# Three linked edits in a four-layer graph network kernel: layer 3's matrix, minus mean over deviation, and the order of work

## The chip, the cores and the metric

The kernel runs on one core of a Trainium2 chip. The metric is the device time of one execution in microseconds (us). Three executions of the kernel before gave 1169.11, 1172.59 and 1173.3 us, so the median is 1172.59 us.

## What is computed

There are 128 graphs of 128 nodes with 128 features. Four layers follow each other, each ending in a residual and a layer norm:

```python
x = _layernorm(x + _L0(x, adj, ...))   # adj @ x + eps0*x, W1 (128x512), rms norm, silu, W2
x = _layernorm(x + _L1(x, ...))        # conv1 (1 tap), conv2 (17 taps), exp(-distance) @ relu(msg), GRU gates
x = _layernorm(x + _L2(x, adj, ...))   # h = x @ W', then 3 hops: adj/row_sum @ ., leaky relu

def _L3_gnn_ref(x, adj, eps, W1, b1, W2, b2):
    aggregated = jnp.einsum('bnm,bmd->bnd', adj, x)
    h = (1.0 + eps) * x + aggregated
    h = jax.nn.relu(h @ W1 + b1)
    return h @ W2 + b2
x = _layernorm(x + _L3(x, adj, ...))
```

`(1+eps)*x + adj @ x` is computed as one product with the matrix `adj + (1+eps)*I`, which is what this document calls layer 3's matrix. A layer norm is applied by ScalarE as `y*rstd + nm`, where `nm` is minus the mean times `rstd`, that is, minus the mean over the deviation.

## The kernel before, in words

Four graphs make a group, and there are 32 groups, numbered k. A tile holds one group: 128 partitions x 512 columns of f32. The program has three phases. Each phase is written as a loop over turns t, and in turn t every engine runs a hand-ordered list of stages, each on its own group: `stage(name, t - d)` works on group t - d if there is such a group. The order of the stages in each engine's list is the order in which that engine executes, and semaphores (`until`, `free`, `landed`) join the lists. So a stage that has to wait holds up everything behind it on its engine. A larger d is a deeper software pipeline: the first turns then have less work and the last ones more.

- **Phase one** (TensorE's loop in lines 534 to 550, 43 turns): layer 0 and the first convolution. `neighbours` (line 417) multiplies with the adjacency matrix to which GpSimd's `add_eps` (1278) has added eps0 times the identity. ScalarE and VectorE split the result into a high and a low part (`high`, `low`) for products of three matmuls (`split_product`, 149). `gram`, `product`, `square_sums`, `mean_square`, `rms`, `spread_rms` make the rms norm, `hidden` and `down` the two weight products, `x1_t`, `conv1` and `transform` what phase two needs. `row_sums` (1041) sums the rows of the adjacency matrix, which is loaded once more as `ad`.
- **Phase two** (568 to 573, 34 pairs of slots): the 17-tap convolution as products in the Fourier domain.
- **Phase three** (733 to 757, 41 turns): layers 1 to 3. `codes`, `distances`, `messages`, `gather` are layer 1's attention-like part, `inverse` returns from the Fourier domain, `hidden_n`, `gate_x`, `gate_nmp`, `gate_conv` make the gates, `y1_t` and `prop_in` start layer 2, `hop1` to `hop3` are its three hops, and `gather3`, `hidden3`, `down3` are layer 3. GpSimd's `add_eps3` (1362) makes layer 3's matrix `at3` from the adjacency matrix `atc` in every turn. VectorE's `moments` and GpSimd's `norm` (1293) give `rstd`, VectorE's `minus_mean` (1223) gives `nm`, and ScalarE's `apply2` (917) and `apply3` (926) apply the norms of layers 2 and 3.

The eight banks of PSUM hold one group's product each and are shared by several stages in turn; the `free(...)` calls say whose reader must be done first. `distances` (591) writes into banks 0 to 3 at once. In the kernel before it waits, through bank 2, for VectorE's `agg3` (1229, tile `agg_lo`, line 1232) of group k - 7:

```python
free(pe, ("agg3_hi agg3_lo", k - 7), ("msg", k), ("z1", k - 8), ("edge", k - 1))
```

VectorE's list in phase three has before that `agg3`, in the same turn: `hop(t-5, 3)`, `points(t, 1)`, `minus_mean(t-6, 0)` and `stats3(t-8)`. All DMAs are issued by SyncE, in one list per phase.

Of the kernel before, what the change touches and what calls it, by code (L numbers as in the profile page):

```python
# [45 lines left out]
ae nb agg agg_hi agg_lo gram prod sums ms r_rms spread rv hid0 hid1 hid2 hid3 hn0 hn1 hn2 hn3  # L46
# [12 lines left out]
y2 moments2 r2 nm2 x3_rows x3b at3 agg3_ps agg3_hi agg3_lo z_ps0 z_ps1 z0 z1 y3_ps y3  # L59
moments3 r3 nm3 out_rows  # L60
# [4 lines left out]
def graph_layers(nc, w, out):  # L65
    with ExitStack() as ctx:
# [6 lines left out]
        X_RING, AT_RING, AD_RING, X1_RING = 4, 2, 2, 2  # L73
# [10 lines left out]
        X1C_RING, ATC_RING, YH_RING, OUT_RING = 4, 8, 2, 2  # L84
# [5 lines left out]
        x1_dram = nc.dram_tensor("x1_scratch", [GROUPS, P, G, P], F32, kind="Internal").ap()  # L90
        yh_dram = nc.dram_tensor("yh_scratch", [SLOTS, B, 2 * P], F32, kind="Internal").ap()
# [89 lines left out]
        eps0_ident = sb("eps0_ident", [P, P])  # L181
# [46 lines left out]
        eps3_ident = sb("eps3_ident", [P, P])  # L228
        one_eps3 = sb("one_eps3", [P, 1])
# [16 lines left out]
        y2, x3_rows, x3b, at3 = rows("y2"), rows("x3_rows"), rows("x3b"), rows("at3")  # L246
# [4 lines left out]
        nm = [sb(f"nm{i}", [P, G]) for i in range(2)]  # L251
# [3 lines left out]
        TURNS1 = GROUPS + 11  # L255
# [7 lines left out]
        DVE_B1_SQ, DVE_BN_VE, DVE_CONV1, DVE_EPS0, DVE_READY = 1, 2, 6, 7, 15  # L263
# [3 lines left out]
        ACT_LATE, DVE_PROP, DVE_LATE = ACT_READY + 4, DVE_TAPS + 10, DVE_TAPS + 14  # L267
# [12 lines left out]
        def everything_first(engine):  # L280
# [23 lines left out]
        def _(sp):  # L304
# [35 lines left out]
            for t in range(TURNS1):  # L340
# [3 lines left out]
                stage(store_x1, t - 6)  # L344
                stage(load_ad, t + 2 - 11)
# [70 lines left out]
        def _(pe):  # L416
            def neighbours(k):
                until(pe, "ae", k)
                landed(pe, x_in, k)
# [1061 lines left out]
```

## Time and profile before

| | |
|---|---|
| median of three executions | 1172.59 us |
| the profiled execution | 1173.6 us |
| its span, first to last instruction | 1171.8 us |
| mean granted TensorE clock | 0.985 |
| busy: TensorE matmul, weight load | 94%, 84% of the span |
| busy: VectorE, ScalarE, GpSimd | 71%, 59%, 48% |
| chain that ended last | TensorE 81%, VectorE 9%, issue 6% |
| read and written in HBM | 55.31 MB, 25.69 MB |

The profiled execution is 1.8 us longer than its span, and 1.0 us over the median. A matmul's duration in the trace includes the pipeline, so matmuls overlap and a TensorE that is shown 100% busy may still have small gaps; distances from start to start tell more. In a timeline row the columns are start, duration (both us), engine, line, operation, tiles and shapes, count, and in square brackets the idle time before it with what ended it.

### The profile page before, as it was taken

Reading aid. Unit: us, or ns where it says so; the run is one execution under the profiler, and the core shown is the slowest. Engines: PE = TensorE matmul, PEld = TensorE weight load, DVE = VectorE, ACT = ScalarE, POOL = GpSimd, SP = SyncE. Lnnn points to the kernel's source line nnn. Section 1 sums busy time; section 2 is a strip of 40 time slices with the busy share of each in tenths; the row PEclk is TensorE's granted clock in tenths of the full one; section 3 lists DMA queues with packets and bytes.
Section 4 is the critical chain, followed back from the end, with each engine's and each line's share of the span. In section 5 each row is a group of like instructions: output and inputs, shape, how many; then the busy total and the mean of one; then the engine's idle time right before and its main releaser. Section 6 shows DMA issues by size and latency. Waiting matters only on the chain.

```text
span 1171.8 us, 25210 instructions
## 1 busy us (share of the span) xinstructions
PE 1102.7 (94%) x8267; PEld 990.0 (84%) x8267; DVE 833.5 (71%) x2596; ACT 694.8 (59%) x1296; POOL 563.0 (48%) x524
## 2 busy tenths in 40 slices
PE   7899999999999789899999999999999999999874
PEld 6799999999999679788888888888888888888774
DVE  4477778787777533146887778877787878877974
ACT  4444555555555332256677777767776776767665
POOL 1244433434342235335555555656555565656654
PEclk9999999999999899899999999999999999999998
DMA  4122332223232255411111121211212121220000
GB/s 156 55 64 75 99 91 91 91 91 91 91 91 64 73 168 180 155 50 58 34 40 54 47 65 47 65 38 47 65 47 65 47 65 40 64 65 10 20 28 36
DMA packets 47110, 82.62 MB, mean 71 GB/s; under 512 B 5316, under 2 KB 15368, under 8 KB 46728
## 3 DMA queue, kind: packets, MB, share of 16 engines
q1 hardware_dynamic: 46984, 81.02, 22.5%
q8 instruction: 69, 1.13, 0.4%
q14 instruction: 57, 0.47, 0.1%
HBM read 55.31 MB, written 25.69 MB: 69 GB/s over the span
## 4 chain that ended last, share of the span: by engine, by line
PE 81%; DVE 9%; issue 6%; ACT 2%; DMA 1%; SPq 0%; POOL 0%; DVEq 0%; POOLq 0%; ACTq 0%
PE banks L156 16%; PE banks L465 9%; PE banks L150 9%; PE banks L151 8%; PE banks L152 8%; PE banks L722 4%; PE banks L631 3%; PE banks L632 3%; PE banks L493 3%; PE banks L558 2%; PE banks L609 2%; PE banks L435 2%; DVE stats L1019 2%; DVE prop L1214 2%; PE banks L587 2%
## 5 line engine op out<-in xcount | busy, mean ns | idle before, releaser
L163 POOL TENSOR_TENSOR rstd<-ve,minus_half 128x4 f32<-128x4 f32 x128 | 130.5, 1020 | 101.9 <-DVE ve L1029 98.8
L163 POOL TENSOR_TENSOR r_rms<-ms,minus_half 128x4 f32<-128x4 f32 x32 | 32.3, 1008 | 224.2 <-DVE ms L993 224.2
L465 PE MATMUL banks<-w,s 128*128 128x128 f32 x768 | 101.2, 275 | 0.4 <-DVE y L1007 0.4
L465 PEld LDWEIGHTS banks<-w,s 128*128 128x128 f32 x768 | 95.6, 192 | 3.4 <-issue 0.5
L150 PE MATMUL banks<-agg_hi,w_hi 128*128 128x512 f32 x192 | 82.4, 429 | 10.1 <-issue 8.6
L1373 POOL TENSOR_TENSOR y<-leaky,x_rows 128x512 f32<-128x512 f32 x32 | 42.6, 1331 | 97.3 <-ACT x_rows L922 96.8
L1019 DVE BATCH_NORM_STATS2 stats<-y 128x6 f32<-128x128 f32 x384 | 82.9, 278 | 1.7 <-POOL y L1373 1.6
L1359 POOL TENSOR_TENSOR x3b<-x_rows,late_rows 128x512 f32<-128x512 f32 x32 | 40.9, 1278 | 82.5 <-DVE y L1239 82.5
L160 ACT ACTIVATE agg_hi<-banks 128x512 fp32r<-128x512 f32 x64 | 38.2, 597 | 64.7 <-PE banks L156 36.1
L151 PE MATMUL banks<-agg_lo,w_hi 128*128 128x512 f32 x192 | 76.4, 398 | 0.0
L152 PE MATMUL banks<-agg_hi,w_lo 128*128 128x512 f32 x192 | 76.3, 398 | 0.0
L156 PE MATMUL banks<-at,x_rows 128*128 128x128 f32 x512 | 69.8, 281 | 4.4 <-DVE agg_lo L981 3.0
L156 PE MATMUL banks<-t,atc 128*128 128x128 f32 x512 | 68.8, 278 | 1.3 <-DVE t L1214 1.3
L722 PE MATMUL banks<-w,z 128*128 128x128 f32 x512 | 69.5, 282 | 0.2
L781 ACT ACTIVATE s<-hn,cols 128x512 f32<-128x512 f32 x96 | 65.0, 712 | 7.7 <-DVE hn L1000 7.7
L1000 DVE SCALAR_TENSOR_TENSOR hn<-banks,cols,rv 128x512 f32<-128x512 f32 x96 | 68.2, 736 | 1.0 <-ACT rv L160 0.6
L156 PEld LDWEIGHTS banks<-at,x_rows 128*128 128x128 f32 x512 | 63.9, 196 | 5.3 <-issue 2.9
L722 PEld LDWEIGHTS banks<-w,z 128*128 128x128 f32 x512 | 64.4, 198 | 1.3 <-ACT z L943 1.3
L156 PEld LDWEIGHTS banks<-t,atc 128*128 128x128 f32 x512 | 63.0, 194 | 1.9 <-DVE t L1214 1.9
L1159 DVE SCALAR_TENSOR_TENSOR c_res<-banks,bn_scale,x1c 128x512 f32<-128x512 f32 x32 | 24.0, 751 | 52.0 <-PE banks L632 52.0
L930 ACT ACTIVATE out_rows<-y,nm,rstd 128x128 f32<-128x128 f32 x128 | 52.5, 483 | 11.8 <-DVE nm L1226 11.7
L1315 POOL TENSOR_SCALAR y<-wh 128x128 f32<-128x128 f32 x67 | 34.3, 530 | 47.8 <-ACT xh L160 25.7
(192 smaller groups left out, 3401.1 us busy)
## 6 DMA issues: line engine op xcount, KB each, us to landing
at<-in_at SPq DMA_DIRECT2D x32, 256.0 KB, 2.9
x_rows<-in_x SPq DMA_DIRECT2D x32, 256.0 KB, 2.9
x_scratch<-x SPq DMA_DIRECT2D x32, 256.0 KB, 3.2
ad<-in_ad SPq DMA_DIRECT2D x32, 256.0 KB, 2.7
x1c<-x_scratch SPq DMA_DIRECT2D x32, 256.0 KB, 2.7
atc<-in_at SPq DMA_DIRECT2D x32, 256.0 KB, 2.9
yh<-yh_scratch SPq DMA_DIRECT2D x32, 256.0 KB
out<-out_rows SPq DMA_DIRECT2D x32, 256.0 KB, 3.1
```

The lines of the kernel that those rows point to most:

```text
L150: pe.matmul(psum, hi, moving_hi, start=start, stop=False)
L151: pe.matmul(psum, hi, moving_lo, start=False, stop=False)
L152: return pe.matmul(psum, lo, moving_hi, start=False, stop=stop)
L156: last = pe.matmul(psum[:, g, :], lhs(g), rhs(g), start=True, stop=True)
L163: return nc.gpsimd.tensor_tensor(to[:], base[:], minus_half[:], ALU.pow)
L465: last = pe.matmul(bank[7][:, g, :], s[c][:, g, :], w2[:, c, :], start=(c == 0 and g == 0), stop=(c == H0 - 1), skip_group_check=True)
L722: last = pe.matmul(bank[6][:, g, :], z3[c][:, g, :], w32[:, c, :], start=(c == 0 and g == 0), stop=(c == H3 - 1), skip_group_check=True)
L781: nc.scalar.activation(s[c][:], hn[c][:], ACT.Silu, scale=column("rms", c)).then_inc(sem[("s0", "s1", "s2", "s3")[c]], 1)
L930: last = nc.scalar.activation(out_rows[k % OUT_RING][:, g, :], y3[:, g, :], ACT.Identity, bias=nm[1][:, g:g + 1], scale=rstd[3][:, g:g + 1])
L1000: V.scalar_tensor_tensor(out=hn[c][:], in0=bank[(5, 0, 1, 3)[c]][:], scalar=column("b1", c), in1=rv[:], op0=ALU.add, op1=ALU.mult).then_in ...
L1019: last = V.bn_stats(stats[n][:, g, :], y[:, g, :])
L1373: Q.tensor_tensor(y2[:], leaky[:], x2_rows[:], ALU.add).then_inc(sem["y2"], 1)
```

## The change

1. Layer 3's matrix. `add_eps3` moves to GpSimd's list of phase one, ahead of `add_eps`, and writes one tile `at3_made`. SyncE stores it to a scratch tensor in HBM (`store_at3`) and loads it back in phase three (`load_at3`) into a ring of two.
2. `minus_mean` moves from VectorE to GpSimd, as two instructions (times -1, then times the mean), each followed by a semaphore.
3. The lists of all engines in phases one and three have another order, with other distances d and another assignment of PSUM banks. Phase one has 42 turns where it had 43. In phase three the gates' products with the neighbours and the convolution go from t - 1 to t - 2, the three hops and layer 3's `hidden3` one turn later too; the number of turns stays 41. Rings: `x1c` 4 to 6, `atc` 8 to 11, `ad` 2 to 1.

The diff, cut to its core (the two small setup instructions for the matrix move with it, and the bank numbers change everywhere):

```diff
-        X_RING, AT_RING, AD_RING, X1_RING = 4, 2, 2, 2
+        X_RING, AT_RING, AD_RING, X1_RING = 4, 2, 1, 2
-        X1C_RING, ATC_RING, YH_RING, OUT_RING = 4, 8, 2, 2
+        X1C_RING, ATC_RING, YH_RING, OUT_RING = 6, 11, 2, 2
-        TURNS1 = GROUPS + 11
+        TURNS1 = GROUPS + 10
...
+            def store_at3(k):
+                until(sp, "at3", k)
+                sp.dma_start(at3_dram[k], at3_made[:]).then_inc(at3_stored, 16)
...
                 stage(load_at, t + 2)
                 if t >= 2:
                     stage(load_x, t + 1)
-                stage(store_x1, t - 6)
-                stage(load_ad, t + 2 - 11)
+                stage(store_at3, t - 0)
+                stage(store_x1, t - 5)
+                stage(load_ad, t + 1 - 9)
...
+            def load_at3(k):
+                until(sp, "agg3_ps", k - 2)
+                landed(sp, at3_in, k - 2)
+                sp.dma_start(at3[k % 2][:], at3_dram[k]).then_inc(at3_in[k % 2], 16)
...
             def distances(k):
                 until(pe, "pts_l", k)
                 until(pe, "pts_r", k)
-                free(pe, ("prop", k - 5), ("v", k - 2), ("edge", k - 1))
-                free(pe, ("factor_r pts_r", k), ("t2", k - 5), ("edge", k - 1))
-                free(pe, ("agg3_hi agg3_lo", k - 7), ("msg", k), ("z1", k - 8), ("edge", k - 1))
-                free(pe, ("xn_hi xn_lo", k - 1), ("z0", k - 8), ("edge", k - 1))
+                free(pe, ("factor_r pts_r", k), ("y3", k - 9), ("edge", k - 1))
+                free(pe, ("tz", k - 2), ("edge", k - 1))
+                free(pe, ("t2", k - 5), ("ht", k - 5), ("edge", k - 1))
+                free(pe, ("ghn", k - 1), ("prop", k - 6), ("t1", k - 6), ("edge", k - 1))
...
             def y1_t(k):
-                free(pe, ("x2_rows", k - 1))
+                free(pe, ("msg", k + 4), ("x2_rows", k - 1))
```

TensorE's new lists, in full:

```python
# phase one
hidden(t-1, 0)  neighbours(t)  square_sums(t-1)  hidden(t-1, 2)  hidden(t-1, 3)  down(t-2, 0)
spread_rms(t-1)  down(t-2, 1)  gram(t)  conv1(t-7)  down(t-2, 2)  transform(t-9, 1)
x1_t(t-4)  hidden(t, 1)  down(t-2, 3)  transform(t-9, 0)
# phase three
codes(t)  hop3(t-6)  gate_nmp(t-2, R)  gate_nmp(t-2, N)  gate_conv(t-2, R)  gate_nmp(t-2, Z)
gate_conv(t-2, N)  hop1(t-5)  hidden_n(t-1)  gate_conv(t-2, Z)  inverse(t)  distances(t)
hidden3(t-8, 0)  gather(t-1)  messages(t)  prop_in(t-4)  y1_t(t-4)  hidden3(t-8, 1)
down3(t-8, 0)  hop2(t-5)  down3(t-8, 1)  gate_x(t-1, Z)  gather3(t-7)  gate_x(t-1, R)
```

VectorE's, ScalarE's and GpSimd's new lists of phase three, and GpSimd's of phase one:

```python
# VectorE
hop(t-6, 3)  agg3(t-8)  points(t, 0)  twice_x(t-3)  moments(t-9, 3)  gate_u(t-2)  points(t, 1)
gate_v(t-2)  hop(t-5, 1)  stats2(t-6)  apply1(t-5)  conv_residual(t)  moments(t-6, 2)
nmp_low(t-1)  stats1(t-4)  moments(t-4, 1)  hop(t-5, 2)  residual3(t-8)  scaled_h(t-4)
twice_n(t-2)  stats3(t-8)
# ScalarE
factors(t, 0)  factors(t, 1)  multiple(t-5, 3)  apply2(t-7)  gate_r(t-2)  leaky_relu(t-6)
multiple(t-5, 2)  hidden_n(t-1)  conv_high(t-1)  gate_z(t-2)  x1_high(t)  multiple(t-5, 0)
edges(t)  nmp_high(t-1)  message(t)  hidden3(t-8, 0)  multiple(t-5, 1)  conv_full(t)
hidden3(t-8, 1)  apply3(t-9)  gate_n(t-2)  agg3(t-7)
# GpSimd
edge_weights(t-1)  residual2(t-6)  x1_low(t)  conv_low(t-1)  norm(t-9, 3)  minus_mean(t-9, 1)
twice_y1(t-3)  norm(t-6, 2)  norm(t-4, 1)  minus_mean(t-6, 0)  x3_bias(t-7)
# GpSimd, phase one
add_eps3(t)  add_eps(t)  rms(t-1)  norm(t-3, 0)  x_bias(t-2)
```

```diff
+            def add_eps3(k):
+                landed(pool, at_in, k)
+                if k >= 1:
+                    pool.wait_ge(at3_stored, 16 * k)
+                Q.tensor_tensor(at3_made[:], at[k % AT_RING][:], over_graphs(eps3_ident), ALU.add
+                                ).then_inc(sem["at3"], 1)
...
+            def minus_mean(k, n):
+                until(pool, ("r2", "r3")[n], k)
+                Q.tensor_scalar(minus_rstd[n][:], rstd[2 + n][:], -1.0, None, ALU.mult
+                                ).then_inc(sem[("minus_r2", "minus_r3")[n]], 1)
+                until(pool, ("minus_r2", "minus_r3")[n], k)
+                Q.tensor_tensor(nm[n][:], minus_rstd[n][:], mv[2 + n][:, :, 0], ALU.mult
+                                ).then_inc(sem[("nm2", "nm3")[n]], 1)
```

VectorE's new list of phase one is `stats0(t-3)`, `mean_square(t-1)`, `moments(t-3, 0)`, `conv1_bias(t-8)`, `low(t)`, `row_sums(t-9)`, `normalise(t-1, 1)`, `normalise(t-1, 0)`, `product(t)`, `normalise(t-1, 3)`, `apply0(t-3)`, `residual0(t-2)`, `normalise(t-1, 2)`.

## Rows read from the trace of the kernel before

**Rows 1.** The page: its span, and busy us (share) and count per engine.
```profile
span 1171.8 us, 25210 instructions
PE 1102.7 (94%) x8267; PEld 990.0 (84%) x8267; DVE 833.5 (71%) x2596; ACT 694.8 (59%) x1296; POOL 563.0 (48%) x524
```

**Rows 2.** Windows: stretch, length, busy PE, PEld, DVE, ACT, POOL, granted clock, DMA share, GB/s.
```profile
29.50:119.10 89.60, 86.55 (x600) 79.08 (x601) 59.92 (x156) 42.62 (x67) 36.02 (x32) 1.00 0.24 68
119.10:373.60 254.50, 254.50 (x1916) 236.52 (x1915) 193.52 (x506) 135.63 (x242) 98.11 (x89) 1.00 0.29 88
373.60:424.30 50.70, 38.02 (x273) 34.77 (x272) 28.02 (x74) 21.71 (x44) 7.44 (x7) 0.93 0.25 81
...
485.10:594.20 109.10, 105.95 (x791) 90.23 (x791) 66.20 (x182) 67.86 (x121) 50.39 (x40) 0.97 0.20 60
594.20:1083.80 489.60, 475.10 (x3602) 418.67 (x3602) 387.72 (x1344) 348.06 (x669) 285.31 (x240) 0.99 0.18 52
1083.80:1171.80 88.00, 62.10 (x411) 55.40 (x409) 65.56 (x268) 53.77 (x109) 47.13 (x40) 0.91 0.08 28
```

**Rows 3.** Timeline of TensorE, phase one: `neighbours` of two turns that follow each other.
```profile
176.92 1.06 PE L156 MATMUL banks<-at,x_rows 128*128 128x128 f32 x8
...
188.49 1.06 PE L156 MATMUL banks<-at,x_rows 128*128 128x128 f32 x8
```

**Rows 4.** Timeline of TensorE, a turn of phase three, from `codes` to `codes`.
```profile
820.43 0.65 PE L587 MATMUL banks<-x1c,code_w 128*32 128x128 f32 x16
...
825.80 1.06 PE L156 MATMUL banks<-t,atc 128*128 128x128 f32 x8
826.70 1.06 PE L156 MATMUL banks<-at,x_rows 128*128 128x128 f32 x8
827.51 0.48 PE L150 MATMUL banks<-x_hi,wt_hi 128*128 128x512 f32 x1
...
828.29 0.40 PE L150 MATMUL banks<-x_hi,wt_hi 128*128 128x512 f32 x1
...
830.15 0.40 PE L152 MATMUL banks<-xn_hi,wt_lo 128*128 128x512 f32 x1
831.13 0.50 PE L600 MATMUL banks<-points_lr 9*128 9x128 f32 x8 [0.57 <-DVE agg_lo L1232]
...
840.67 0.53 PE L587 MATMUL banks<-x1c,code_w 128*32 128x128 f32 x12
```

**Rows 5.** Line 600 (`distances`): what ended its waits, us and times.
```profile
  DVE agg_lo L1232: 14.5, 24
```

**Rows 6.** Timeline of VectorE ahead of that wait.
```profile
828.20 1.20 DVE L1226 SCALAR_TENSOR_TENSOR nm<-mv,rstd 128x4 f32<-128x4 f32 x1
```

**Rows 7.** Timeline of TensorE: a stretch at the lower clock in phase three.
```profile
647.88 1.91 PE L156 MATMUL banks<-w3h,atc 128*128 128x128 f32 x8
```

**Rows 8.** Tile `nm`: VectorE's `minus_mean`, ns min/median/max, first and last start.
```profile
L1226 DVE SCALAR_TENSOR_TENSOR nm<-mv,rstd x64: 143/191/1235, 566.9 to 1167.5; 128x4 f32<-128x4 f32 x64
```

**Rows 9.** The page, costliest groups: GpSimd's power on 128x4, and its one-input 128x128.
```profile
L163 POOL TENSOR_TENSOR rstd<-ve,minus_half 128x4 f32<-128x4 f32 x128 | 130.5, 1020 | 101.9 <-DVE ve L1029 98.8
...
L1315 POOL TENSOR_SCALAR y<-wh 128x128 f32<-128x128 f32 x67 | 34.3, 530 | 47.8 <-ACT xh L160 25.7
```

**Rows 10.** Groups by line, GpSimd, 800 to 1000 us: `add_eps3`.
```profile
L1365 POOL TENSOR_TENSOR at<-atc,eps_ident 128x512 f32<-128x512 f32 x9 | 11.6, 1288 | 0.0
```

**Rows 11.** DMA issues: count, KB each, median us from issue to landing.
```profile
x_scratch<-x SPq DMA_DIRECT2D x32, 256.0 KB, 3.2
ad<-in_ad SPq DMA_DIRECT2D x32, 256.0 KB, 2.7
```

**Rows 12.** Timeline of TensorE, last turns of phase one.
```profile
410.29 1.13 PE L156 MATMUL banks<-conv_w,x 128*128 128x128 f32 x8 [1.67 <-DVE hcp L1039]
...
414.02 1.13 PE L156 MATMUL banks<-conv_w,x 128*128 128x128 f32 x8 [1.67 <-DVE hcp L1039]
```

**Rows 13.** Timeline of TensorE, first turn of phase three: `inverse`.
```profile
490.71 0.69 PE L631 MATMUL banks<-idft,yh 68*128 68x128 f32 x2 [1.41 <-DMA yh<-yh_scratch]
```

More of the change, by code:

```diff
@@ L245, in graph_layers @@
         t2, t1, prop, leaky = rows("t2"), rows("t1"), rows("prop"), rows("leaky")
-        y2, x3_rows, x3b, at3 = rows("y2"), rows("x3_rows"), rows("x3b"), rows("at3")
+        y2, x3_rows, x3b = rows("y2"), rows("x3_rows"), rows("x3b")
+        at3 = [rows(f"at3_{i}") for i in range(2)]
         agg3_hi, agg3_lo = rows("agg3_hi", F32R), rows("agg3_lo", F32R)
@@ L432, in square_sums @@
                 until(pe, "prod", k)
-                free(pe, ("xh1", k - 9), ("hn2", k - 1), ("ms", k - 1))
+                free(pe, ("y0", k - 2), ("ms", k - 1))
                 for g in range(G):
-                    last = pe.matmul(bank[1][:, 0, g:g + 1], agg[:, g, :], ones[:, 0:1], start=True, stop=True)
+                    last = pe.matmul(bank[0][:, 0, g:g + 1], agg[:, g, :], ones[:, 0:1], start=True, stop=True)
                 last.then_inc(sem["sums"], 1)
@@ L462, in down @@
                 if c == 0:
-                    free(pe, ("y0", k - 1))
+                    free(pe, ("ms", k + 1), ("y0", k - 1))
                 for g in range(G):
-                    last = pe.matmul(bank[7][:, g, :], s[c][:, g, :], w2[:, c, :], start=(c == 0 and g == 0),
+                    last = pe.matmul(bank[0][:, g, :], s[c][:, g, :], w2[:, c, :], start=(c == 0 and g == 0),
                                      stop=(c == H0 - 1), skip_group_check=True)
@@ L550, in _ @@
                 stage(down, t - 2, 1)
+                stage(gram, t)
+                stage(conv1, t - 7)
+                stage(down, t - 2, 2)
+                stage(transform, t - 9, 1)
+                stage(x1_t, t - 4)
+                stage(hidden, t, 1)
+                stage(down, t - 2, 3)
+                stage(transform, t - 9, 0)
             def slot_product(psum, slot):
@@ L719, in down3 @@
                 if c == 0:
-                    free(pe, ("c2_res", k + 7), ("ghn", k + 6), ("y3", k - 1))
+                    free(pe, ("edge", k + 8), ("factor_r pts_r", k + 8), ("y3", k - 1))
                 for g in range(G):
-                    last = pe.matmul(bank[6][:, g, :], z3[c][:, g, :], w32[:, c, :], start=(c == 0 and g == 0),
+                    last = pe.matmul(bank[0][:, g, :], z3[c][:, g, :], w32[:, c, :], start=(c == 0 and g == 0),
                                      stop=(c == H3 - 1), skip_group_check=True)
@@ L1038, in conv1_bias @@
                 until(dve, "hc", k - 1)
-                V.tensor_tensor(hcp[:], bank[4][:], over_graphs(conv1_b), ALU.add).then_inc(sem["hcp"], 1)
+                V.tensor_tensor(hcp[:], bank[6][:], over_graphs(conv1_b), ALU.add).then_inc(sem["hcp"], 1)
             def row_sums(k):
```

360 lines of the change are left out of this document (173 added, 187 removed).

## The prediction

> **What bounds the kernel now.** I read the page first: TensorE is busy for 94% of the span, VectorE for 71%, ScalarE for 59%, GpSimd for 48% [rows 1]. So time can come only from TensorE's work, from its gaps, or from the ends of the phases. The windows by stretch split the span into phase one's first ten turns (89.60 us), its full turns (254.50) and its last turns (50.70), then, after phase two (from 424.30 to 485.10), phase three's first eight turns (109.10), its 24 full turns (489.60) and its end (88.00) [rows 2]. 29.5 us of set-up come before them. In phase one's full turns TensorE is busy all the time, 254.50 of 254.50 [rows 2], and two starts of `neighbours` are 188.49 - 176.92 = 11.57 us apart [rows 3]. Reading one such turn from start to start I found no gap: 11.57 us is TensorE's own work, and no order makes it shorter.
>
> In phase three a turn takes 840.67 - 820.43 = 20.24 us [rows 4], and there is a gap. The last matmul before `distances` starts at 830.15 and `distances` at 831.13 [rows 4], 0.98 us, where neighbours of that kind follow in 0.23 (828.29 is three matmuls after 827.51, at 0.32 + 0.23 + 0.23). So 0.74 us are lost in each of the 24 full turns. What ended them is VectorE's `agg_lo`, 24 times, 14.5 us as the profile counts idle time [rows 5]. Ahead of `agg_lo` VectorE ran `minus_mean`, a 128x4 instruction that took 1.20 us [rows 6]; the same instruction takes 0.143 at best and 1.235 at worst [rows 8]. I looked at all 64: in every full turn the one for layer 2 takes 1.18 to 1.20, the one for layer 3 0.15. The long one of [rows 6] runs until a GpSimd instruction of 1.3 us, which had started 0.12 before it, ends. That is 1.05 us in VectorE's queue right ahead of what TensorE waits for, more than the 0.74 lost.
>
> **The change part by part.**
>
> *Phase three, full turns.* In the new lists `distances` no longer waits for layer 3's `agg_lo`; bank 6 holds that. I laid the new TensorE list out against the clock with the old steps: a fp32 product of eight matmuls 0.90 (825.80 to 826.70), 0.81 before a split product, a split product 0.78 after fp32 and 0.70 after another [rows 4]. The change of kind costs nothing on balance (0.08 more on one side, 0.09 less on the other), although there are seven such changes in the new list where there were three. The sum of one turn is 20.24 - 0.74 = 19.5 us, as before without the gap. Then I laid the other engines beside it, offsets from `codes`. ScalarE: `factors` to 1.5, `multiple` 2.1, `apply2` 3.7, `gate_r` 4.5 when its product ends, `leaky` 5.0, `hidden_n` 7.5, `conv_high` 8.1, `gate_z` 8.7. `distances` is due at 9.2 and needs `tz`: 0.4 us to spare. VectorE: `hop3` to 2.8, `agg3` 3.3, `points` done by 5.7 (3.5 to spare), `apply1` 9.4 where `messages` at 11.3 needs it, `hop2` 17.6, last `stats3` 20.2, that is 0.7 into the next turn, where `hop3` is not ready before 1.7. GpSimd is idle for some 4 us. The tightest joint is bank 7: `y1_t` is due at 13.4 and `message`, which must have emptied the bank, ends at 13.3. I take 0.05 for it. So 24 turns x 19.55 = 469.2 in place of 489.60, and of this stretch's two spells at the lower clock (one starts at 647.88, where eight matmuls take 1.91 instead of 1.06 [rows 7]; granted clock 0.99 [rows 2]; 1.75 us each in the length of their turns) I keep one: 471, **-18.6 us**, from 0 (another gap of the same size) to -21 (no gap, no such spell).
>
> *minus_mean on GpSimd.* VectorE loses 0.15 + 1.20 a turn. GpSimd gains four small instructions. The trace has no such one: the nearest are the power on 128x4, 1.02, and a one-input 128x128, 0.53 [rows 9]. I take 0.5 each, 2.0 a turn; at 1.02 it is 4.1. Against it stands `add_eps3`, 1.29, which leaves phase three [rows 10]. With 1.02 each, `nm` for `apply2` is ready 0.7 into the turn and wanted at 2.1, so at either price it is covered in a full turn. Not in the last turn of the program, where `moments`, `norm`, `nm`, `apply3`, store follow each other: there it costs 0.9 to 1.9 us. The second of them waits for the first on the same engine, a semaphore's time, inside these prices.
>
> The Trainium skill (SBUF - State Buffer, section on who interferes with whom) says that GpSimd and a VectorE instruction with two inputs in SBUF lock each other out of a shared port for the whole instruction. The trace agrees: `minus_mean` is such an instruction, and lasts 1.20 or 0.15 as GpSimd is busy or not. By that rule VectorE's `gate_u`, `twice_x` and `twice_n` can be held up too; that is priced below as a rival.
>
> *Layer 3's matrix in phase one.* GpSimd gets 1.29 us a turn more [rows 10], on 98.11 us busy of 254.50 [rows 2], and it writes before `neighbours(t)` can start. The loop is: `neighbours(t)` ends, SyncE issues `load_at`, `load_x` and `store_at3` (0.4 to 0.5 each), the store lands 3.2 after its issue (the like store of x1, [rows 11]), `add_eps3(t+1)` 1.29, `add_eps(t+1)` 1.3. That is 0.2 + 1.0 + 3.2 + 2.6 + 0.9 for `neighbours` itself, 7.9 us, under 11.57: nothing in full turns, with `x_bias`, `norm` and `rms` done before. In turns 1 and 2, which are shorter than that, it costs some 2 us. The store and the reload add 8.4 MB each; DMA engines are busy for 29% of phase one and 18% of phase three [rows 2], and SyncE's list waits for nothing new that TensorE needs within a turn. Nothing.
>
> *Phase one's order.* The pipeline is one turn shallower, so early turns hold more work. With the same unit steps the new turns 0 to 9 are 6.4, 7.1, 9.5, 9.4, 9.9, 9.9, 9.9, 10.8, 10.8 and 11.6 = 95.3, and 2 for the store loop, 97.5 against 89.60: **+8**. Full turns: the same work; `square_sums` loses a start that a split product before it gave (0.08 a turn at most): 22 turns, 0 to +1.8, I take **+1**. End: before, 50.70 us with TensorE at clock 0.93 [rows 2]; its late turns are a loop of 3.72 us (410.29 to 414.02) in which `conv1` waits 1.67 for VectorE's `hcp` [rows 12]. New: two turns of 9.3 and 7.2 with layer 0's rest, one of 4.9, then turns of 4.2. These last are now set by `ad`, whose ring of one makes load (2.7, [rows 11]), issue and row sum (0.68) a loop of 4.2 and stands ahead of `hcp` in VectorE's list. 9.3 + 7.2 + 4.9 + 4 x 4.2 + 4.5 = 42.7: **-8**, from -12 to 0. Phase two: same work, **0**.
>
> *Phase three's ends.* Start: the first turn gets worse, since `inverse` waits for its data until 490.71 [rows 13] and `distances` and `messages`, which were done in that wait, now stand behind it: 11 us for 9.2. The turns after hold less (gates one turn later): 7.2, 11.7, 11.7, 13.0, 14.8, 15.7, 16.6. Sum 101.7 against 109.10: **-7.4**, from -10 to -3. End: the 8.9 us of work that the start lost come here, 63 us of TensorE work where there were 54. I went through the nine turns: 15.4, 12.5, 12.8, 11.6, 8.8, 7.2, 5.8, and 13.4 for the last group to its store, 87.5 us, against 88.00. The old turns waited for VectorE, which waited for GpSimd's `norm` before `minus_mean`; the new ones are full with work. A clock of 0.91 [rows 2] and joints that I drew without slack make it worse: I take **+1.5**, from -3 to +8.
>
> **Sum.** +8 + 1 - 8 + 0 - 7.4 - 18.6 + 1.5 = -23.5 us. The profiled execution took 1173.6 (span 1171.8 and 1.8 around it), which is 1.0 above the median of 1172.6. So 1149 us.
>
> **The rivals.**
> - *The gap only moves* (12%). In place of `agg_lo`, `distances` waits for `tz`, or `y1_t` for `message`, for 0.7 us in each full turn. For it: 0.4 and 0.1 us to spare in a plan by hand, six more semaphore joints on TensorE. Against: ScalarE has 14 us of work in 19.5. Then the 18.6 shrink to 2, and the time is 1173 - 7 = 1166.
> - *Ports* (8%, inside the forecast's range). GpSimd holds up `twice_x` and `gate_u` by 1.2 us each. `apply1` then ends at 11.8, and `messages`, due at 11.3, waits 0.5: 24 x 0.5 = 12 us, 1161. Against: GpSimd waits for `leaky` in just that stretch. By the skill's rule above this is where it would bite.
> - *Slower than before* (7%): ScalarE's queue before `gate_z`. `apply2` waits for `nm` from GpSimd, and behind it stand `gate_r`, `leaky`, `hidden_n`, `conv_high`, `gate_z`, and for `tz` the whole of TensorE. If `nm` comes 1.4 + 0.4 + x us later than I have it, each full turn loses x. To eat the 23.5 us, x must be 1.0 us over 24 turns; at x = 1.4 the time is 1173 - 23.5 + 34 = 1183. That needs 3 us more on GpSimd than at the highest price of the trace.
> - *The ends give more* (8%): no lower clock in the late turns, `ad` hidden, shorter joints: -12 more, 1137.
> - *The change does not do what it says*: the gap's cause stays because another stage waits for `agg3`. In the new lists `hidden3` does, 6 us later. I give it nothing of its own.
>
> **How the numbers follow.** Forecast as summed: 65%, about 1149, by itself 1141 to 1158. The range reaches to the gap that only moves and to most of the better ends: 1137 to 1166. A measurement of this kernel tells about 0.5% from no change, 5.9 us. Under 1166.7 lie the forecast, the ports, the better ends and half of the moved gap, 0.86; within 5.9 of the old time the rest of the moved gap and a little of the bad tail, 0.08; slower 0.06.
>
> **What would show it.** Right: TensorE's starts of `codes` 19.5 to 19.6 us apart in turns 8 to 31 and no idle time ahead of `distances`; `minus_mean` short on GpSimd, 0.5 or less each; phase two's first matmul near 425 us; the last `codes` about 26 us earlier. Wrong: turns above 20, a wait of TensorE for ScalarE's `tz` or `message`, an end of phase one over 48 us, or an end of phase three over 95.

## The result, and the profile after

The changed kernel takes 1163.78 us (median of 20 executions, 1162.28 to 1169.23), the kernel before beside it 1172.94 (20 executions). The ratio is 0.9935, 95% interval 0.9922 to 0.9949: 9.2 us less. The forecast was 23.5 us less. The sign and the range held; the size did not. Three of the runs below had one execution each that took far longer (1599, 3141 and 2213 us), which their medians and ratios leave out.

The page of the changed kernel ([rows 1] has that of the kernel before):

```profile
span 1162.0 us, 25279 instructions
PE 1102.8 (95%) x8267; PEld 993.2 (85%) x8267; DVE 805.2 (69%) x2532; ACT 701.2 (60%) x1296; POOL 604.2 (52%) x652
```

TensorE's busy time is what it was. VectorE has 28 us less. GpSimd has 41 us more: 27.7 are the 128 small instructions of part 2 (by the groups of GpSimd, 64 of 0.233 and 64 of 0.201 us), 15.3 are two old instructions that take longer in the new order, `edge_weights` (1.63 us for 1.29) and `residual2` (1.47 for 1.33); others are a little shorter.

The same stretches as [rows 2], in the windows view of the changed kernel (stretch, length, busy PE, PEld, DVE, ACT, POOL, granted clock, DMA share, GB/s). Phase two is here too:

```profile
29.60:127.10 97.50, 93.86 (x644) 85.22 (x645) 63.21 (x167) 45.30 (x73) 51.67 (x44) 1.00 0.29 95
127.10:381.60 254.50, 254.50 (x1915) 239.40 (x1915) 187.91 (x507) 135.48 (x243) 124.90 (x108) 1.00 0.34 112
381.60:425.80 44.20, 30.70 (x228) 28.20 (x228) 22.44 (x63) 18.56 (x39) 6.65 (x7) 0.96 0.24 78
425.80:486.40 60.60, 59.50 (x407) 55.82 (x407) 17.07 (x30) 12.10 (x21) 34.98 (x69) 1.00 0.53 182
486.40:589.90 103.50, 98.33 (x740) 83.79 (x741) 53.98 (x154) 61.98 (x107) 42.95 (x37) 0.95 0.26 79
589.90:1062.90 473.00, 472.71 (x3602) 418.08 (x3602) 375.28 (x1289) 353.49 (x670) 289.54 (x313) 1.00 0.20 64
1062.90:1162.00 99.10, 72.37 (x462) 63.30 (x460) 70.18 (x286) 61.21 (x122) 49.83 (x68) 0.91 0.12 41
```

Set against [rows 2] and against the terms of the sum:

| stretch | before | after | difference | forecast |
|---|---|---|---|---|
| phase one, first ten turns | 89.60 | 97.50 | +7.9 | +8 |
| phase one, full turns | 254.50 | 254.50 | 0 | +1 |
| phase one, end | 50.70 | 44.20 | -6.5 | -8 |
| phase two | 60.80 | 60.60 | -0.2 | 0 |
| phase three, start | 109.10 | 103.50 | -5.6 | -7.4 |
| phase three, 24 full turns | 489.60 | 473.00 | -16.6 | -18.6 |
| phase three, end | 88.00 | 99.10 | **+11.1** | **+1.5** |

Six of the seven terms are within 2 us of what was summed. The last is off by 9.6 us, two thirds of the miss of 14.3 (23.5 less 9.2). Most of the rest lies in the end of phase one and in phase three's start and full turns, 1.5 to 2.0 us too little gain in each. The signs that the prediction had named point the same way: right were no wait ahead of `distances` and phase two from 425.8 us; short were turns of 19.69 us for 19.5 to 19.6 and the last `codes` 20.4 us earlier for 26; and an end of phase three over 95 us had been named as a sign of being wrong.

The gap is gone. TensorE's timeline of a full turn, from `codes` (line 601) over the last of `inverse` and `distances` (line 614) to the next `codes`, answers to [rows 4]:

```profile
806.61 0.65 PE L601 MATMUL banks<-x1c,code_w 128*32 128x128 f32 x16
...
815.55 0.39 PE L646 MATMUL banks<-idft,yh 68*128 68x128 f32 x2
815.90 0.50 PE L614 MATMUL banks<-points_lr 9*128 9x128 f32 x8
816.33 0.50 PE L152 MATMUL banks<-agg_hi,w_hi 128*128 128x512 f32 x1
...
826.30 0.64 PE L601 MATMUL banks<-x1c,code_w 128*32 128x128 f32 x16
```

`distances` starts 0.35 us after the last pair of `inverse`, with no wait shown, where it had been 0.98. The turn is 826.30 - 806.61 = 19.69 us. The two small instructions of `minus_mean` on GpSimd (tile view, ns min/median/max; [rows 8] has the one of before):

```profile
L1315 POOL TENSOR_SCALAR minus_rstd<-rstd x64: 228/230/245, 574.3 to 1157.4; 128x4 f32<-128x4 f32 x64
L1318 POOL TENSOR_TENSOR nm<-minus_rstd,mv x64: 199/200/204, 574.6 to 1157.7; 128x4 f32<-128x4 f32 x64
```

### The profile page after: what moved, and what is told of

Same layout as the page of the kernel before. It is cut to its first block, busy times and chain, and to the rows that moved or that the text cites. A ratio compares the mean times of both kernels' runs of the same rounds, so it can differ in the third digit from the quotient of the medians.

```text
span 1162.0 us, 25279 instructions
## 1 busy us (share of the span) xinstructions
PE 1102.8 (95%) x8267; PEld 993.2 (85%) x8267; DVE 805.2 (69%) x2532; ACT 701.2 (60%) x1296; POOL 604.2 (52%) x652
## 4 chain that ended last, share of the span: by engine, by line
PE 89%; DVE 3%; POOL 2%; issue 2%; ACT 2%; DMA 2%; SPq 0%; ACTq 0%; POOLq 0%; DVEq 0%
PE banks L158 19%; PE banks L152 11%; PE banks L153 10%; PE banks L154 10%; PE banks L479 10%; PE banks L736 4%; PE banks L645 3%; PE banks L646 3%; PE banks L623 3%; PE banks L572 3%; PE banks L507 2%; PE banks L449 2%; PE banks L601 2%; PE banks L686 1%; PE banks L539 1%
## 5 line engine op out<-in xcount | busy, mean ns | idle before, releaser
L1357 POOL TENSOR_TENSOR x_lo<-x1c,x_hi 128x512 fp32r<-128x512 f32 x32 | 41.1, 1284 | 114.6 <-ACT x_hi L162 114.6
L1390 POOL TENSOR_TENSOR y<-leaky,x_rows 128x512 f32<-128x512 f32 x32 | 46.9, 1466 | 102.2 <-ACT leaky L929 102.2
L152 PE MATMUL banks<-agg_hi,w_hi 128*128 128x512 f32 x192 | 90.0, 469 | 9.8 <-issue 8.3
L158 PEld LDWEIGHTS banks<-at,x_rows 128*128 128x128 f32 x512 | 67.7, 195 | 7.7 <-POOL at L1295 1.7
L795 ACT ACTIVATE s<-hn,cols 128x512 f32<-128x512 f32 x96 | 67.7, 713 | 7.6 <-DVE hn L1014 7.6
L1289 POOL TENSOR_TENSOR at_made<-at,eps_ident 128x512 f32<-128x512 f32 x32 | 41.1, 1285 | 37.0 <-DMA at_scratch<-at_made 26.4
L1027 DVE TENSOR_SCALAR x_rows<-y,mv,rstd 128x128 f32<-128x128 f32 x128 | 36.1, 345 | 29.8 <-PE banks L490 29.8
```

The source lines that it names most:

```text
L152: pe.matmul(psum, hi, moving_hi, start=start, stop=False)
L158: last = pe.matmul(psum[:, g, :], lhs(g), rhs(g), start=True, stop=True)
L795: nc.scalar.activation(s[c][:], hn[c][:], ACT.Silu, scale=column("rms", c)).then_inc(sem[("s0", "s1", "s2", "s3")[c]], 1)
L1289: Q.tensor_tensor(at3_made[:], at[k % AT_RING][:], over_graphs(eps3_ident), ALU.add).then_inc(sem["at3"], 1)
L1390: Q.tensor_tensor(y2[:], leaky[:], x2_rows[:], ALU.add).then_inc(sem["y2"], 1)
```

## The experiments

Two questions: which part of the change closes the gap, and what makes the end of phase three 11 us longer. Each run is compared with the kernel before on the same chip, so between groups of runs that were made at different times it is the ratios that compare.

### The gap: one stage moved

```diff
-                stage(minus_mean, t - 6, 0)
                 stage(stats3, t - 8)
                 stage(agg3, t - 7)
+                stage(minus_mean, t - 6, 0)
```

> The kernel before with one stage moved: in VectorE's list of phase three `minus_mean(t-6, 0)` stands behind `stats3(t-8)` and `agg3(t-7)` instead of ahead of them. Nothing else changes. If the 0.74 us gap ahead of `distances` is the 1.20 us that the long `minus_mean` takes in VectorE's queue [rows 5, 6], the gap closes in all 24 full turns: turns of 19.5 to 19.7 us in place of 20.24, 13 to 18 us in all, about 1156. If the gap was set by something else in the order of the work (the banks, ScalarE's `agg3_hi`), another wait takes its place: turns above 20.0, 1168 to 1174.

Measured: 1158.19 us, ratio 0.9861 (0.9838 to 0.9884). Full turns of 19.59 us, TensorE busy for all of them (windows view), while the long `minus_mean` is still there (VectorE's timeline), now behind `agg_lo`; TensorE's timeline shows `distances` 0.32 us after the matmul before it:

```profile
595.50:1065.60 470.10, 470.10 (x3602) 414.99 (x3602) 383.08 (x1344) 347.49 (x670) 284.31 (x240) 1.00 0.18 54
...
819.49 0.68 DVE L1232 TENSOR_TENSOR agg_lo<-banks,agg_hi 128x512 fp32r<-128x512 f32 x1
820.08 1.08 DVE L1226 SCALAR_TENSOR_TENSOR nm<-mv,rstd 128x4 f32<-128x4 f32 x1
...
820.68 0.39 PE L152 MATMUL banks<-xn_hi,wt_lo 128*128 128x512 f32 x1
821.00 0.50 PE L600 MATMUL banks<-points_lr 9*128 9x128 f32 x8
```

So a long `minus_mean`, here 1.08 us in a full turn, costs nothing once it stands behind `agg_lo`. It was its place in VectorE's queue that made the gap. That one moved line gives more than the whole change.

### The gap: part 2 alone

`minus_mean` leaves VectorE's list, and in GpSimd's list of the kernel before stand:

```diff
                 stage(norm, t - 6, 2)
+                stage(minus_mean, t - 6, 0)
...
                 stage(norm, t - 8, 3)
+                stage(minus_mean, t - 8, 1)
```

> The kernel before with part 2 alone: `minus_mean` on GpSimd, each right behind its `norm`. Theory 1 (the long `minus_mean` in VectorE's queue makes the gap): turns of 19.5 to 19.7 us, 1154 to 1159, within 3 us of the run with `minus_mean` moved later; the end of phase three within 1 us of the 88.0 us of before, since two GpSimd instructions of 0.23 and 0.20 us in place of one of 0.15 on VectorE cost 0.3 us in the last turn. Theory 2 (the new order of all lists removes the gap): no change, 1170 to 1174. Theory 3 (work taken to GpSimd delays GpSimd's other stages): slower than 1174.

Measured: 1152.86 us, ratio 0.9814 (0.9789 to 0.9838), 1 us under the first theory's range. Theories 2 and 3 are out. The stretches of its phase three, start, full turns and end:

```profile
486.80:596.20 109.40, 105.91 (x791) 90.17 (x791) 66.17 (x180) 67.80 (x121) 51.23 (x44) 0.97 0.20 60
596.20:1066.40 470.20, 470.20 (x3602) 415.06 (x3602) 369.38 (x1297) 347.55 (x670) 304.84 (x336) 1.00 0.18 54
1066.40:1152.40 86.00, 60.70 (x410) 54.01 (x408) 59.86 (x253) 53.29 (x109) 52.47 (x69) 0.94 0.08 28
```

470.20 against 489.60 [rows 2], the start as before, the end 2.0 us shorter. The small instructions on GpSimd cost nothing that shows. The time is 5.3 us under that of the line moved later, where 3 at most were expected. Nearly all of it is the end of phase three, 86.0 us here and 90.8 there, with granted clocks of 0.94 and 0.90; why that end is longer no run looks into. Phase three is 665.6 us here and 675.6 in the changed kernel: the new order is 10 us longer than the old one once the gap is closed by part 2, namely 13.1 us in the end and 2.8 in the full turns, less 5.9 gained at the start.

### The gap: part 2 undone in the changed kernel

`minus_mean` is back on VectorE. In the first try layer 3's stood behind `gate_v`:

```diff
                 stage(gate_v, t - 2)
+                stage(minus_mean, t - 9, 1)
...
                 stage(hop, t - 5, 2)
+                stage(minus_mean, t - 6, 0)
```

> The changed kernel with part 2 undone: `minus_mean` back on VectorE as one instruction, in the changed order (layer 2's behind `hop(t-5, 2)`, layer 3's behind `gate_v(t-2)`). Theory A (in the changed order the gap ahead of `distances` is gone whatever `minus_mean` does, since bank 6 holds layer 3's product): turns stay at 19.7 us and the time within 3 us of the changed kernel's 1163.8. Theory B (the lock on the long `minus_mean` comes back somewhere in VectorE's queue and is seen by TensorE): up to 1.0 us a turn, up to 1180.

Measured: 1352.17 us, ratio 1.1534 (1.1506 to 1.1563). Neither theory had this. VectorE's and TensorE's timelines of one turn:

```profile
900.35 0.16 DVE L1241 SCALAR_TENSOR_TENSOR nm<-mv,rstd 128x4 f32<-128x4 f32 x1 [6.67 <-POOL rstd L165]
...
901.84 0.81 PE L614 MATMUL banks<-points_lr 9*128 9x128 f32 x8 [5.18 <-DVE t L1229]
```

GpSimd's `norm(t-9, 3)` stands behind `residual2`, `x1_low` and `conv_low` in its list, late in the turn. VectorE waited for it for 6.67 us, and `distances` for `t2` behind it for 5.18; turns were 27.3 us. So an instruction of 0.16 us holds its queue for forty times as long as it runs, because of where another engine's list puts its operand. The second try moves that stage behind `moments(t-4, 1)`:

> The changed kernel with part 2 undone as in after_nm_vector, but `minus_mean(t-9, 1)` behind `moments(t-4, 1)` in VectorE's list instead of behind `gate_v(t-2)`, where it waited 6.67 us in each turn for GpSimd's `rstd` and made turns of 27.3 us. Theory A (the changed order removes the gap by itself): turns of 19.7 us and 1162 to 1166. Theory B (the long `minus_mean` is seen again in some place): 19.8 to 20.7, 1167 to 1188. If A holds, parts 2 and 3 each remove the gap and are worth it only once.

Measured: 1165.16 us, ratio 0.9948 (0.9924 to 0.9972), which overlaps the changed kernel's. Theory A holds. Windows and tile:

```profile
595.20:1068.20 473.00, 472.72 (x3603) 418.11 (x3602) 379.40 (x1336) 356.11 (x670) 267.88 (x217) 1.00 0.20 64
...
L1241 DVE SCALAR_TENSOR_TENSOR nm<-mv,rstd x64: 149/160/220, 579.1 to 1162.9; 128x4 f32<-128x4 f32 x64
```

The full turns are 473.00 us, equal to the changed kernel's. Here `minus_mean` never meets a long GpSimd instruction (0.22 us at most), so this run doesn't say what a held one would cost in the new order. But parts 2 and 3 each close the gap without the other, and what it cost (489.60 less 473.00, or less 470.20 in the old order) comes only once.

### Part 1 alone

`add_eps3`, its store and its reload are added to the kernel before as in the diff above, ahead of `add_eps` in GpSimd's list and behind `load_x` in SyncE's, with the order of before; `add_eps3` leaves phase three, and `ad` has a ring of one and is loaded a turn later.

> The kernel before with part 1 alone: layer 3's matrix made by GpSimd in phase one, stored, and loaded back in phase three into a ring of two; the order of the stages is that of before (`ad` has a ring of one and is loaded one turn later, for the memory). It takes 1.29 us a turn from GpSimd in phase three, and GpSimd's instruction is what holds `minus_mean`. Theory 1 (the lock on `minus_mean` is `twice_y1`, which stays): the gap stays, phase three is unchanged, phase one's first two turns 1 to 2 us longer: 1172 to 1176. Rival (with `add_eps3` gone GpSimd runs `twice_y1` earlier, and it no longer meets `minus_mean`): turns of 19.5 us and 1156.

Measured: 1224.35 us, ratio 1.0424 (1.0400 to 1.0448), 50 us slower, which neither theory had. In phase three the first one held: turns of 20.24 us, 24 waits of `distances` for `agg_lo` (13.8 us), and a `minus_mean` of 1.19 us beside `twice_y1`; the rival is out. The loss is in phase one, half of it in its first ten turns (115.4 us for 89.6) and half in its full turns, which are 12.7 us instead of 11.57. SyncE's, GpSimd's and TensorE's timelines of one such turn:

```profile
246.49 0.33 SPq L317 DMA_DIRECT2D at<-in_at  x1
251.61 0.33 SPq L313 DMA_DIRECT2D x_rows<-in_x  x1
251.98 0.44 SPq L325 DMA_DIRECT2D at_scratch<-at_made  x1
...
255.39 1.27 POOL L1297 TENSOR_TENSOR at_made<-at,eps_ident 128x512 f32<-128x512 f32 x1 [0.65 <-DMA at_scratch<-at_made]
256.74 1.26 POOL L1303 TENSOR_TENSOR at<-at,eps_ident 128x512 f32<-128x512 f32 x1
...
258.06 1.16 PE L158 MATMUL banks<-at,x_rows 128*128 128x128 f32 x8 [0.94 <-POOL at L1303]
```

`load_x` waits for `y0` (as it does in the kernel before, where only the store of x1 stands behind it and nothing is late), and the store of the matrix stands behind it: issued at 251.98, 5.5 us after `load_at`, it lands 3.3 us later, and then GpSimd needs 2.6 us until `neighbours` can start. The load of `ad` is not in this loop: it was issued at 257.42, and `load_at` behind it only at 259.25, when `neighbours` had ended. In the changed kernel `load_x` is issued right behind `load_at`; there `residual0`, which makes `y0`, comes a turn earlier (SyncE again):

```profile
243.91 0.33 SPq L317 DMA_DIRECT2D at<-in_at  x1
244.35 0.37 SPq L313 DMA_DIRECT2D x_rows<-in_x  x1
244.76 0.43 SPq L325 DMA_DIRECT2D at_scratch<-at_made  x1
```

So part 1 needs phase one's new order, and the prediction's loop of 7.9 us can hold only for that order.

### Part 1 undone in the changed kernel

The matrix is made in phase three again, and phase one has its new order without the store:

```diff
                 stage(edge_weights, t - 1)
+                stage(add_eps3, t - 7)
                 stage(residual2, t - 6)
...
```

> The changed kernel with part 1 undone: GpSimd makes layer 3's matrix in phase three, between `edge_weights(t-1)` and `residual2(t-6)`, where it is idle for some 3 us in a full turn. If part 1 is worth nothing in either phase: 1160 to 1165, phase one some 1 us shorter in its first turns (97.5 to 96). If GpSimd's 1.29 us a turn back in phase three delays `residual2` or `twice_y1` so that TensorE sees it: turns above 19.8 us, 1166 to 1180.

Measured: 1165.47 us, ratio 0.9932 (0.9905 to 0.9959), no difference from the changed kernel's 0.9935. Its full turns are 19.70 us. Its first ten turns of phase one took 95.4 us, and 97.50 with the matrix. The next run, also without the matrix, took 96.4 for them, so the store loop costs 1 to 2 us, about what the prediction gave it. The matrix on GpSimd had been covered in phase three, so that moving it gains nothing.

### Phase one's order alone

The kernel before with the lists, banks and distances of phase one from the diff, without the matrix.

> The kernel before with phase one's order, banks and number of turns from the changed kernel, without the matrix in phase one. Phase one there took 97.50 + 254.50 + 44.20 us against 89.60 + 254.50 + 50.70. If the order does it and the store loop of the matrix costs nothing: +1.4 us, 1174 to 1175. If the store loop costs the 2 us that the prediction gave it in turns 1 and 2: -0.6 us, 1172 to 1173. Phase three is as before, with its gap.

Measured: 1172.41 us, ratio 0.9988 (0.9969 to 1.0007): no difference that can be told, so executions don't decide between the two sums that were expected. It agrees with the table, where phase one's +7.9 and -6.5 nearly cancel.

### The end: other banks in the late turns

```diff
+        LATE = 30
...
+        def y1_bank(k):
+            return 4 if k == LATE else 7
...
+        def in_bank(k):
+            return 1 if k >= LATE else 2
...
             def y1_t(k):
                 until(pe, "y1", k)
-                free(pe, ("msg", k + 4), ("x2_rows", k - 1))
+                if k == LATE:
+                    free(pe, ("v", GROUPS - 1))
+                else:
+                    free(pe, ("msg", k + 4), ("x2_rows", k - 2 if k > LATE else k - 1))
...
             def prop_in(k):
                 until(pe, "y1", k)
-                free(pe, ("edge", k + 4), ("t2", k - 1), ("ht", k - 1))
...
+                if k >= LATE:
+                    free(pe, ("tz", GROUPS - 1))
+                    free(pe, ("ht", k - 1))
+                else:
+                    free(pe, ("edge", k + 4), ("t2", k - 1), ("ht", k - 1))
...
```

> The changed kernel with other banks in its late turns alone: `prop_in` of groups 30 and 31 goes to bank 1 and `y1_t` of group 30 to bank 4, both free once the gates have ended; so `prop_in` no longer waits for `t2` of the group before (1.89 and 1.64 us), nor `y1_t` for `x2_rows` in that turn. Theory Tb (shared banks make the end long): the turns of `gather3` that took 15.55 and 15.43 us become 12 to 14, the end of phase three 93 to 96 in place of 99.1, time 1158 to 1161. Theory Td (VectorE's chain of the late turns, `hop2` after `t2`, sets them, whatever bank): the waits move from `prop_in` to `hop2`, time 1162 to 1165.

Measured: 1157.73 us, ratio 0.9880 (0.9854 to 0.9906), below the changed kernel's interval. What it cures, in TensorE's timeline of the changed kernel (turns 34 and 35):

```profile
1093.36 1.13 PE L158 MATMUL banks<-w3h,atc 128*128 128x128 f32 x8 [0.54 <-issue]
1096.38 0.47 PE L152 MATMUL banks<-agg_hi,w_hi 128*128 128x512 f32 x1 [1.88 <-issue]
...
1099.21 2.05 PE L158 MATMUL banks<-prop_w,y 128*128 128x128 f32 x8 [1.89 <-DVE t L1229]
...
1113.14 1.13 PE L158 MATMUL banks<-prop_w,y 128*128 128x128 f32 x8 [1.64 <-DVE t L1229]
1115.19 1.09 PE L686 MATMUL banks<-ident,y 128*128 128x128 f32 x4 [0.92 <-DVE x_rows L1212]
...
1117.36 1.91 PE L736 MATMUL banks<-w,z 128*128 128x128 f32 x8
1119.06 1.92 PE L158 MATMUL banks<-t,atc 128*128 128x128 f32 x8
```

`prop_in` (1099.21, 1113.14) waits for VectorE's `t2` of the group before, because `hop1` (1093.36), whose product `t2` is made from, and `prop_in` both use bank 2. In a full turn 6.6 us of other products lie between `hop1` and `prop_in`; when the gates have ended, only the three matmuls of `hidden3` do (1096.38). Behind `prop_in` stand `y1_t`, `hidden3`, `down3` and `hop2`, and VectorE waits for the last of these. With the other banks neither `prop_in` waits; the first still runs at the lower clock (1.83 us for 1.05), behind the wait of 1.88 that stays:

```profile
1097.82 1.83 PE L158 MATMUL banks<-prop_w,y 128*128 128x128 f32 x8
...
1109.22 1.05 PE L158 MATMUL banks<-prop_w,y 128*128 128x128 f32 x8
```

From `gather3` to `gather3` turns 34 to 36 took 15.55, 15.43 and 9.32 us, and now take 12.59, 9.80 and 10.97. The end of phase three as in the table:

```profile
1063.60:1155.80 92.20, 69.69 (x462) 61.50 (x460) 69.83 (x286) 61.23 (x122) 49.89 (x68) 0.95 0.14 44
```

92.20 for 99.10, that is 6.9 of the 9.6 us by which the term was off. Theory Td, that no bank matters, is out. A part of it remains: in turn 36, which got 1.65 us longer, TensorE waits 1.04 us for VectorE.

### The end: the clock

```diff
+            def filler():
+                until(pe, "tz", GROUPS - 1)
+                for i in range(12):
+                    pe.transpose(bank[1][:, 0, :], ident[:], ident[:])
...
+                if t in (34, 35):
+                    filler()
                 stage(hidden3, t - 8, 0)
                 stage(gather, t - 1)
                 stage(messages, t)
+                if t in (34, 35):
+                    filler()
                 stage(prop_in, t - 4)
```

> The changed kernel with twelve extra transposes of the identity into the unused bank 1 ahead of `hidden3(t-8, 0)` and again ahead of `prop_in(t-4)`, in turns 34 and 35 alone, where TensorE waited 0.5 to 2.2 us; their result is not read. Theory Ta (the two spells at the lower clock, granted clock 0.78 in both turns, make the loss): the clock stays at 1.00 there, `prop_in` takes 1.1 and not 2.05 us, and the end is 4 to 6 us shorter, 1158 to 1160. Rival (the spells fall in stretches that wait for VectorE anyway, or come back a turn later): within 1.5 us of the changed kernel, or slower by what the extra work costs, up to 2 us.

Measured: 1160.96 us, ratio 0.9906 (0.9878 to 0.9934). The windows of turns 34 and 35, in the changed kernel and then in this one, with the granted clock third from the end:

```profile
1090.90:1106.40 15.50, 11.19 (x68) 9.85 (x67) 12.74 (x49) 8.63 (x17) 8.64 (x13) 0.78 0.11 35
1106.40:1121.90 15.50, 11.88 (x69) 10.66 (x69) 10.48 (x48) 8.19 (x16) 6.42 (x9) 0.78 0.15 51
```
```profile
1091.60:1105.80 14.20, 11.58 (x92) 10.53 (x91) 12.77 (x49) 8.64 (x17) 7.97 (x11) 1.00 0.12 39
1105.80:1118.40 12.60, 11.15 (x92) 10.51 (x91) 10.25 (x47) 8.19 (x16) 7.15 (x12) 1.00 0.12 43
```

In turn 34 of the changed kernel TensorE waited 0.54, 1.88 and 1.89 us, one after the other, and the clock fell to its lower level, 1.2 GHz: `prop_in` took 2.05 us instead of 1.1 (the granted clock of 0.78 is the mean over both levels). With extra work in those waits it stayed at 2.4 GHz, and the two turns are 4.2 us shorter although `prop_in` still waited 0.60 and `y1_t` 0.92. The end is 95.1 us, 4.0 less, the lower edge of what Ta expected. The ratio's interval overlaps the changed kernel's, so executions alone don't show the gain; the trace carries this. The two causes overlap: the bank makes the waits, the waits bring the lower clock, and the other banks cure most of both. So their gains, 6.9 and 4.0 us, are not to be added.

### The end: a second y3

To the kernel with other banks a ring of two for `y3` is added; `residual3` then waits for `out_rows` of group k - 2.

> after_late_banks with a second buffer for `y3` as well, so that `residual3` of a group doesn't wait for `apply3` of the group before. In the changed kernel that wait was 1.88 us in turn 38 (y3 at 1140.94), and `agg_lo`, for which `hidden3` waits, stood behind it. Theory Tc (the single `y3` and the late `nm3` add to the end): that turn is 1 to 2 us shorter, 1.0 to 2.0 us less than after_late_banks, 1156.5 to 1157.5. Rival (`agg3_hi` stands behind the same `apply3` on ScalarE, and takes its place): within 0.5 us of after_late_banks.

Measured: 1155.93 us, ratio 0.9879 (0.9843 to 0.9915); against 0.9880 without the ring there is no difference that executions can tell. In the trace the turn in question, `gather3` to `gather3`, is 7.54 us instead of 8.59, which is the 1 us expected, and the end 90.9. That is within 1.4 us of the prediction's 89.5, though not by the same turns: the fifth is now 10.97 us where 8.8 was planned.

### Putting together what pays

First, the kernel before with part 2 and phase one's order:

> The kernel before with two parts of the change and nothing else: `minus_mean` on GpSimd, and phase one's order and banks; phase three keeps its order, and the matrix stays in phase three. If the parts add up: before_nm_gpsimd's 1152.9 less 1.4 us, that is 1151 to 1152, about 12 us under the changed kernel. If phase one's order gives nothing on its own (its run was within 0.1% of before): 1152.5 to 1154.

Measured: 1152.33 us, ratio 0.9845 (0.9804 to 0.9886); this agrees with part 2 alone (0.9814), and phase one's order adds nothing that can be told. Then a swap in the late turns:

```diff
-                stage(y1_t, t - 3)
-                stage(hop2, t - 4)
+                if t >= 33:
+                    stage(hop2, t - 4)
+                    stage(y1_t, t - 3)
+                else:
+                    stage(y1_t, t - 3)
+                    stage(hop2, t - 4)
```

> nm_and_phase1 with one more edit, in the late turns alone (t of 33 and more): `hop2(t-4)` ahead of `y1_t(t-3)`, since there `y1_t` waited 2.74 and 2.56 us for VectorE's `x2_rows` with `hop2`'s operand ready. If VectorE's chain through `t1` sets these turns: 1 to 3 us less than nm_and_phase1. If `stats1` behind `y1_t` sets them: no change, or up to 1 us more.

Measured: 1149.76 us, ratio 0.9840 (0.9798 to 0.9883): no difference that can be told. The late turns 34 to 38 sum to 50.5 us instead of 51.7, which is less than two traces of the same late turns differ by: turn 34 took 13.74 us with part 2 alone and 12.11 with phase one's order beside it. So the swap is not decided. No version is clearly better than the kernel before with `minus_mean` on GpSimd and nothing else, 1.9% under before and 1.2% under the change.

## Why the prediction was right or wrong

*What bounds the kernel.* Right. The gap was `minus_mean` ahead of `agg_lo`: moving that stage alone gave turns of 19.59 us.

*Full turns.* Forecast 19.55 us and one spell at the lower clock, 471; measured 19.69, no spell, 473.0. The sum was 0.14 us a turn too low, for two reasons. The gap was sized at 0.74 us, since `distances` was taken to follow a split product in 0.23; without the gap it follows in 0.32 (820.68 to 821.00), so 0.66 were lost, and the order of before without them has 19.59 where 19.5 was taken. And the new order takes 0.10 more than that. Its TensorE has no wait, so this lies in the steps between kinds of product (0.35 from the last pair of `inverse` to `distances`), which the prediction set off at zero; no run isolates them. Neither the moved gap nor the late `apply2` of the rivals came: TensorE is busy for 472.71 of 473.00 us. The bound for bank 7 (`y1_t` after `message`) was not reached: no wait there.

*minus_mean on GpSimd.* 0.23 and 0.20 us where 0.5 was taken and 1.02 was the bound. In the last group the way from the start of GpSimd's power to `apply3` is 1.67 us, before 1.24, so it costs 0.4 us once. The rival "ports" had the right mechanism: beside GpSimd's `x3_bias` and `edge_weights`, VectorE's `twice_n` takes 1.47 us in a full turn where it took 0.69 before, and `edge_weights` itself is longer too. That is what the Trainium skill says (SBUF - State Buffer, "Who interferes with whom"), and the trace agrees. In full turns it falls where TensorE waits for neither. In turn 34 it does not: VectorE's queue runs with no idle time from `twice_n` to the `t2` for which `prop_in` waits 1.89 us, and two of its instructions last longer than in a turn where they are free, 1.45 for 0.69 and 0.84 for 0.17 (VectorE's timeline):

```profile
1092.42 1.45 DVE L1201 SCALAR_TENSOR_TENSOR yb<-tz,nn 128x512 f32<-128x512 f32 x1
...
1097.20 0.84 DVE L1043 TENSOR_SCALAR ve<-mv 128x4 f32<-128x4 f32 x1
1097.95 1.11 DVE L1229 SCALAR_TENSOR_TENSOR t<-banks,row_inv,w2h 128x128 f32<-128x128 f32 x4
```

GpSimd's `x3_bias` and `residual2` run beside the two. By these rows up to 1.4 us of that one wait may come from there, an estimate that no run tests.

*Layer 3's matrix.* The store loop cost 1 to 2 us for the 2 that were taken (97.50 against 96.4 and 95.4 without it). "Nothing in full turns" was right for the new order. The step that made it right, that `load_x` ahead of the store waits for nothing, was not stated, and in the old order it is false and costs 50 us.

*Phase one's order.* +7.9, 0 and -6.5 for +8, +1 and -8. The late turns stayed at 3.72 us, as in [rows 12]:

```profile
411.69 1.13 PE L158 MATMUL banks<-conv_w,x 128*128 128x128 f32 x8 [1.67 <-DVE hcp L1053]
415.41 1.13 PE L158 MATMUL banks<-conv_w,x 128*128 128x128 f32 x8 [1.67 <-DVE hcp L1053]
```

So the `ad` ring of one, which was to make them 4.2, doesn't set them, and the loss against the forecast lies in the rest of that stretch.

*Phase three's end: the failed step.* The prediction said: "I went through the nine turns: 15.4, 12.5, 12.8, 11.6, 8.8, 7.2, 5.8, and 13.4", and took +1.5, from -3 to +8. Measured, from `gather3` to `gather3`, were 15.28, 14.39, 15.55, 15.43, 9.32, 7.53 and 8.61, and 14.7 from the last one to the end (the first of them starts 1.7 us ahead of the stretch of 99.10). The term came to +11.1, beyond the bound. It said "the new ones are full with work", and that failed: TensorE is busy for 72.37 of 99.10 us. The prediction costed TensorE's work and VectorE's chain, but not the waits for a bank that the new assignment adds, which in the late turns lose their cover, nor the lower clock that they bring. With these waits away the third and fourth turn are 12.59 and 9.80, under the forecast's, and the end is 6.9 us shorter. The second turn's 14.39 is mostly more work (13.43 us busy) than was counted. Of the seventh's 8.61, 2.8 over the forecast, 1.1 us is `y3` waiting for `out_rows`; the rest was not tested. The lower clock had been named as a risk, without a number.

That the time still lies in the range is luck. Its upper edge, 1166, was the price of a gap that only moves, which did not happen; what filled that room was the end of phase three, which the prediction had bounded at +8.

*What was not asked.* The sum counted the gains of parts 2 and 3 as one gap, which was right, but nowhere does it say what part 2 would give alone, for which [rows 5, 6] were enough. Against part 2 alone the new order of phase three is worth -5.9 at the start, +2.8 in the full turns and +13.1 at the end.

## What to carry to other kernels

When a stage stands in a queue ahead of what the bounding engine waits for, try first to move that one stage; here it gave 1.4% and moving it to another engine 1.9%, while the change with all lists in a new order kept only a third of that. When a software pipeline is redrawn, go through the last turns with the list of bank and buffer waits in hand and not only the work, since a wait that is covered in full turns is bare when the stages between have ended. And a store added to an engine's list of DMAs inherits the waits of the loads ahead of it, here the wait of `load_x`, by which the store went out 5.5 us behind `load_at`.

## What the runs showed of the hardware

A VectorE instruction with two inputs on 128x4 took 0.15 us alone and up to 1.23 where it started while a GpSimd instruction of 1.3 us was running, and the same arithmetic as two instructions on GpSimd took 0.43 us in all, less than half of the 1.02 us of the power on the same shape. And TensorE's clock fell to 1.2 GHz after three waits of 0.5 to 1.9 us close together, where twelve transposes of unused data in each of two waits kept it at 2.4 GHz and made the turns 4.2 us shorter.
